# A windowed-attention block on one core: fc2 rows moved into the attention loop, value products for two pairs at once

## The reference

```
y   = layernorm(x) * g1 + b1, rolled by (-3, -3), cut into 64 windows of 49 tokens per image
qkv = y @ qkv_w.T + qkv_b                                  # 3 x 16 heads x 8
a   = softmax(q @ k.T / sqrt(8) + rel_pos_bias + shift_mask)
x1  = x + roll_back((a @ v) @ proj_w.T + proj_b)
out = x1 + (gelu((layernorm(x1) * g2 + b2) @ fc1_w.T + fc1_b)) @ fc2_w.T + fc2_b     # 128 -> 512 -> 128
```

## Time and profile before

| | us |
|---|---|
| median of three runs | 4173.44 |
| the profiled execution | 4173.6 |
| its span, first to last instruction | 4171.8 |
| PE busy | 3995.3 (96%) |
| DVE busy | 2933.7 (70%) |
| ACT busy | 2726.8 (65%) |
| POOL busy | 2122.9 (51%) |

### The profile page before, as it was taken

How to read it: one execution, slowest core, us unless ns; L and a number is a source line. 1 busy time by engine, 2 the same in 40 slices (tenths; PEclk the granted TensorE clock), 3 DMA queues, 4 the chain that set the end, 5 groups by cost and what they waited for, 6 DMA issues and landing times.

```text
span 4171.8 us, 170732 instructions
## 1 busy us (share of the span) xinstructions
PE 3995.3 (96%) x72080; PEld 3128.2 (75%) x72080; DVE 2933.7 (70%) x7196; ACT 2726.8 (65%) x5120; POOL 2122.9 (51%) x3476
## 2 busy tenths in 40 slices
PE   3899999999999999999999999999999999999998
PEld 2677777777777777777777777777777777777777
DVE  6677777777767777776777777777677767777774
ACT  1566666666666666666666666666666666666665
POOL 4455555555555555555555555555555455555553
PEclk8999999999999999999999999999999999999999
DMA  2333333333333333333333333333333333333332
GB/s 74 103 107 109 106 110 107 110 107 107 111 103 109 110 107 108 107 111 106 109 107 107 108 109 110 108 106 112 102 110 107 111 103 108 108 108 108 110 111 59
DMA packets 625966, 441.61 MB, mean 106 GB/s; under 512 B 158468, under 2 KB 624756, under 8 KB 625204
## 3 DMA queue, kind: packets, MB, share of 16 engines
q1 hardware_dynamic: 624739, 428.88, 34.8%
q0 software_dynamic: 464, 1.81, 0.1%
HBM read 106.14 MB, written 51.46 MB: 38 GB/s over the span
## 4 chain that ended last, share of the span: by engine, by line
PE 54%; ACT 16%; DVE 10%; issue 9%; DMA 7%; SPq 2%; ACTq 0%; POOL 0%; DVEq 0%; POOLq 0%
PE ps L766 13%; PE ps L718 10%; PE ps L796 9%; DMA sums<-pv_sb 7%; PE ps L753 7%; PE ps L748 6%; PE ps L780 6%; ACT hid L425 5%; ACT v_own L482 5%; DVE k_lo L615 3%; DVE yT_lo L600 3%; ACT probs L408 3%; ACT k_hi L466 2%; SPq L248 2%; DVE q_lo L615 2%
## 5 line engine op out<-in xcount | busy, mean ns | idle before, releaser
L570 DVE TENSOR_REDUCE neg_max<-ps 113x16 f32<-113x784 f32 x1024 | 993.1, 970 | 394.7 <-PE ps L718 386.1
L408 ACT ACTIVATE probs<-ps 113x784 f32<-113x784 f32 x1024 | 831.4, 824 | 492.8 <-PE ps L753 489.5
L796 PE MATMUL ps<-w,hid 128*112 128x128 f32 x7168 | 858.3, 274 | 0.0
L796 PEld LDWEIGHTS ps<-w,hid 128*112 128x112 f32 x7168 | 815.2, 177 | 21.9 <-issue 0.2
L753 PE MATMUL ps<-st_q,st_k 128*49 128x196 f16 x8192 | 700.9, 249 | 0.0
L748 PE MATMUL ps<-bias,eye_k 108*64 108x392 f16 x4096 | 689.8, 332 | 0.6 <-DMA bias<-neg_maxT 0.6
L425 ACT ACTIVATE hid<-ps,col 128x448 f32<-128x448 f32 (+1 forms) x1024 | 511.9, 576 | 231.1 <-PE ps L780 231.1
L766 PE MATMUL ps<-probs,v_own 113*32 113x49 f32 x32768 | 576.5, 210 | 45.0 <-ACT probs L408 34.3
L766 PEld LDWEIGHTS ps<-probs,v_own 113*32 113x32 f32 x32768 | 432.0, 109 | 227.7 <-issue 132.3
L378 POOL TENSOR_TENSOR x_b<-x,fc_b 112x896 f32<-112x896 f32 x128 | 267.7, 2091 | 604.4 <-DVE y_out L563 604.4
L718 PE MATMUL ps<-mx_k,mx_q 128*49 128x196 f16 x8192 | 548.7, 254 | 17.8 <-DMA mx_k<-k_hi 8.8
(11 more groups left out here) (108 smaller groups left out, 6962.8 us busy)
## 6 DMA issues: line engine op xcount, KB each, us to landing
st_k<-k_hi SPq DMA_DIRECT2D x256, 196.0 KB
st_q<-q_hi SPq DMA_DIRECT2D x1024, 49.0 KB
oT_raw<-pv_sb SPq DMA_DIRECT2D x256, 196.0 KB, 2.7
x_in<-in_x SPq DMA_DIRECT2D x224, 196.0 KB
x_res<-in_x SPq DMA_DIRECT2D x224, 196.0 KB
out_y<-y_out SPq DMA_DIRECT2D x224, 196.0 KB
mx_q<-q_hi SPq DMA_DIRECT2D x128, 196.0 KB
mx_k<-k_hi SPq DMA_DIRECT2D x512, 49.0 KB
```

Source lines behind the costliest of these rows:

```text
L408: nc.scalar.activation(probs[0:KP, w % 2, :].rearrange("p (b c) -> p b c", b=2), ps[0:KP, b:b + 2, 0:HB * WT], ACT.Exp).then_inc(s_exp, 1)
L570: nc.vector.tensor_reduce(neg_max[0:KP, :, w, :], ps[0:KP, 0:2, 0:HB * WT].rearrange("p b (h k) -> p b h k", k=WT), AX_X, ALU.max, negate= ...
L796: last = mm(tokens_of(6)[0:TP, i, :], hid[:, c, i * TP:(i + 1) * TP], w_2[:, c, :], start=(c == 0), stop=(c == CH - 1))
```

## The change

The mathematics stays the same. What moves:

- **fc2 and its evacuation.** `HALVES` is replaced for fc2 by `FC2_PARTS` = rows 0 to 2 and rows 3 to 6. Rows 3 to 6 of step t-2 run in the attention loop of turn t, one at each odd w, ahead of `max_logits`; rows 0 to 2 run in the head of the next turn. Each part uses bank 7 alone. The final addition of rows 3 to 6 is at the end of DVE's turn.
- **pv.** Two pairs' value products are one group of 32 matmuls in bank 6, at w = 2, 4, 6 and in the next head, with one copy of 392 columns instead of two of 196. Four probability buffers replace two.
- **The head's order.** The transposes of z are first, ahead of pv. Then come x's transposes, the maxima's, three fc2 rows, two fc1 groups, k, q, one fc1 group, the spread, the last fc1 group, v, the output projection. fc1 and gelu work on 784 columns in two banks, in four groups instead of eight. The k and q copies on ACT take both images at once.
- **yT.** The high part is written by ACT straight from PSUM, the low part by DVE from PSUM; the float32 copy and the cast on DVE go.
- **The row maxima in the logits.** They were two rows of the `bias` operand and are now the unused fourth row of each group of `st_q`, against ones in `st_k`; bias no longer has a copy for each w. The four DMAs of the maxima carry 32 pieces of 98 values each instead of 64 of 49.
- **SP.** The store `out_y` is issued after the maxima, ahead of `r_rows`, instead of after the logits' operands.
- **DVE.** `norm1` runs before k_lo and q_lo instead of after them.

```diff
@@ SP body
+                n = t - 3
+                if exists(n):
+                    sp.wait_ge(s_fin, 2 * (n + 1))
+                    band_dmas(sp, outr, y_out, n, edge(n), True, s_stored)
                 n = t - 1
                 if exists(n):
...
-                n = t - 3
-                if exists(n):
-                    sp.wait_ge(s_fin, 2 * (n + 1))
-                    band_dmas(sp, outr, y_out, n, edge(n), True, s_stored)
@@ ACT
+            def gelu(n, c):
+                if c == 0 and past(n, 0):
+                    act.wait_ge(s_fc2, 2 * n)
+                act.wait_ge(s_fc1, CH * n + c + 1)
+                bank = 2 + 2 * (c % 2)
+                nc.scalar.activation(hid[:, c, :].rearrange("p (b q) -> p b q", b=2), ps[:, bank:bank + 2, 0:HT],
                                      ACT.Gelu, bias=col[:, BF + c:BF + c + 1], scale=1 / W_SCALE).then_inc(s_gelu, 1)
...
                     for w in range(NW):
                         exp_pair(t, w)
-                        if w > 0:
-                            copy_pv(t, w - 1)
+                        if w % 2 == 0 and w > 0:
+                            copy_pv(t, w // 2 - 1)
@@ DVE body
                 if exists(t - 3):
                     finish(t - 3, 0, edge)
                 n = t + 2
                 if exists(n) and n != 0:
                     norm1(n, edge)
-                if exists(t - 3):
-                    finish(t - 3, 1, edge)
+                n = t + 1
+                if exists(n):
+                    for j, (hi, lo, bank, b) in enumerate(((k_hi, k_lo, 0, BK), (q_hi, q_lo, 6, BQ))):
+                        dve.wait_ge(s_hi, 2 * n + j + 1)
+                        for im in range(2):
+                            last = nc.vector.scalar_tensor_tensor(
...
+                if exists(t - 2):
+                    finish(t - 2, 1, edge)
@@ PE
+            def pv(n, u):
+                pe.wait_ge(s_exp, NW * n + 2 * u + 2)
...
+                for w in (2 * u, 2 * u + 1):
+                    for h in range(NH):
+                        g, r = h // NR, h % NR
+                        first = (2 * g + w % 2) * WT
+                        last = mm(ps[32 * r:32 * r + VC, 6, first:first + WT],
+                                  v_own[0:KP, w, h, :], probs[0:KP, w % 4, h * WT:(h + 1) * WT], start=True, stop=True)
...
+            def fc2(n, p, i):
+                first, end = FC2_PARTS[p]
+                if i == first and p == 1:
+                    pe.wait_ge(s_gelu, CH * (n + 1))
...
+                for c in range(CH):
+                    last = mm(ps[0:TP, 7, (i - first) * C:(i - first + 1) * C], hid[:, c, i * TP:(i + 1) * TP], w_2[:, c, :],
+                              start=(c == 0), stop=(c == CH - 1))
...
                 for w in range(NW):
                     if exists(t):
                         logits(t, w, edge, odd(0))
-                    if exists(t) and w > 0:
-                        pv(t, w - 1)
+                        if w % 2 == 0 and w > 0:
+                            pv(t, w // 2 - 1)
+                    if exists(t - 2) and w % 2:
+                        fc2(t - 2, 1, FC2_PARTS[1][0] + w // 2)
                     if exists(t + 1):
                         max_logits(t + 1, w, edge)
```

More of the change, by code:

```diff
@@ L261, in body @@
                     sp.wait_ge(s_negT, n + 1)
[L262 to L266, removed]
+                    for e in range(EQ):
+                        row = 32 * e + MAX_ROW
+                        sp.dma_start(st_q[odd(0)][row:row + 1, e, :, :].rearrange("p g c -> p (g c)"),
+                                     neg_maxT[32 * e:32 * (e + 1), :, :]).then_inc(s_neg_dma, 16)
+                n = t - 3
+                if exists(n):
+                    sp.wait_ge(s_fin, 2 * (n + 1))
+                    band_dmas(sp, outr, y_out, n, edge(n), True, s_stored)
                 n = t - 1
@@ L779, in fc1 @@
+            def fc1(n, c):
+                if c == 0:
+                    pe.wait_ge(s_h_lo, n + 1)
+                elif c == 1 and exists(n + 1):
+                    pe.wait_ge(s_exp, NW * (n + 2))
+                elif c > 1:
+                    pe.wait_ge(s_gelu, CH * n + c - 1)
+                bank = 2 + 2 * (c % 2)
                 for k, (ww, hh) in enumerate(((w1_hi, h_hi), (w1_hi, h_lo), (w1_lo, h_hi))):
-                    last = mm(ps[:, 2 + m % 4, 0:(i1 - i0) * TP], ww[:, c * C:(c + 1) * C], hh[:, i0 * TP:i1 * TP],
-                              start=(k == 0), stop=(k == 2))
+                    for b in range(2):
+                        last = mm(ps[:, bank + b, 0:HT], ww[:, c * C:(c + 1) * C], hh[:, b * HT:(b + 1) * HT],
+                                  start=(k == 0), stop=(k == 2))
@@ new lines, in body @@
+            def body(t, edge, odd):
+                n = t - 2
+                if exists(n):
+                    pe.wait_ge(s_z2, n + 1)
+                    if exists(t - 1):
+                        pe.wait_ge(s_exp, NW * t - 1)
+                    else:
+                        pe.wait_ge(s_gelu, CH * n)
+                    for i in range(WS):
+                        last = nc.tensor.transpose(tokens_of(2)[:, i, 0:TP], z2[:, i, :], idn[0:TP, 0:TP])
+                    last.then_inc(s_t2, 1)
@@ L802, in body @@
                 if exists(t - 1):
[L803 to L805 removed]
+                    pv(t - 1, NU - 1)
                 n = t + 1
@@ L815, in body @@
                     max_transposed(t)
-                n = t - 2
-                if exists(n):
-                    pe.wait_ge(s_z2, n + 1)
-                    if not exists(t - 1):
-                        pe.wait_ge(s_gelu, 2 * CH * n)
-                    for i in range(WS):
-                        last = nc.tensor.transpose(tokens_of(2)[:, i, 0:TP], z2[:, i, :], idn[0:TP, 0:TP])
-                    last.then_inc(s_t2, 1)
-                if exists(t - 3):
-                    fc2(t - 3, 2, 4)
+                if exists(t - 3):
+                    for i in range(*FC2_PARTS[0]):
+                        fc2(t - 3, 0, i)
@@ L839, in body @@
                 if exists(t - 2):
-                    for m in range(4):
-                        fc1(t - 2, m)
-                if exists(t - 3):
-                    fc2(t - 3, 4, WS)
+                    fc1(t - 2, 2)
                 n = t - 1
```

337 lines of the change are left out of this document (159 added, 178 removed).

## The result

The changed kernel takes **4627.6 us** (median of 4 runs, 4616.4 to 4649.1) against 4173.6 us: ratio 1.109, interval 1.107 to 1.111. It is 454 us slower. The forecast was 4795 us, range 4440 to 4930, slower. The profiled execution took 4637.0 us, with a span of 4635.2.

What follows compares the result with a forecast made beforehand. It took PE's own work to bound the loop, and put two chains' wait at the changed kernel's spread: 4173.6 + 124 x (3.24 turn + 1.8 clock) = 4799, say 4795 us; range 4440 to 4930, its own 4690 to 4930.

Steps and rivals of the forecast that it cites:

- PE ready for the spread at 10.3: In the head, PE finishes all work ahead of the spread 10.3 us into the turn.
- r_rows at 15.0: SP's chain to the spread: r_rows lands 15.0 us into the turn, including 3.7 to land and 0.6 for out_y ahead.
- The rule that I weighed: A DMA's semaphore lands after that engine's earlier writes: r_rows behind out_y, spread at 15.6, 0.5 us more per turn.
- k_lo at 15.6 (14.1 if x_in is early): DVE's chain to the spread: x_in at 12.3, statistics 2.07, k_lo 1.16; done at 15.6, or 14.1 with early x_in.
- The spread at 15.1: In the head, the spread starts 15.1 us into the turn (14.1 to 16.2), PE idling 4.8 us before it.
- The loop at 15.3: PE's attention loop with four fc2 rows in it takes 15.3 us per turn.
- The turn at full clock, 34.85: The whole turn without clock loss: 15.1 + 4.45 + 15.3 = 34.85 us, 3.2 more than before.
- The clock, 1.8 per turn: After the idle stretch at the spread, PE's lower clock adds 1.8 us per turn, bounds 1.7 and 5.
- The sum: Over 124 turns, 3.24 us of longer turn plus 1.8 for the clock adds 625 us.
- The same waits, the clock stays up: Rival: the spread waits as forecast but the clock does not fall; 4575 us (4450 to 4710), 36%.
- No wait, 3981: Rival: no wait at the spread, the loop and fewer gaps save 1.55 us per turn; 3981 us, 9%.
- the clock stays low, 5195: Rival: the clock stays low through the head and part of the loop, 5 us per turn; 5195 us, 6%.

Runs made afterwards that it cites:

- e1: The changed kernel with the store out_y put back behind the logits' operands on SP: 4540.8 us, ratio 1.087.
- e2: The changed kernel with the statistics of x_in put back behind k_lo and q_lo: 4668.4 us, median of three, ratio 1.116.
- e3: The changed kernel with both moves undone, out_y behind the logits' operands and the statistics of x_in behind k_lo and q_lo: 4321.0 us, ratio 1.035.
- e8: The kernel of e4 with the maxima's DMAs sent to two neighbouring unread rows of the value tile, maxima left out of the logits: 4890.9 us, one run.
- e4: The changed kernel with each of the four maxima's DMAs carrying 64 pieces of 98 bytes instead of 32 of 196: 4657.3 us, ratio 1.115.
- e5: The changed kernel with twelve superfluous fc1 matmuls, 2.0 us, added on PE just ahead of the spread: 4457.5 us, ratio 1.068.
- e10: The changed kernel with all seven fc2 rows in the head, rows 3 to 6 ahead of k, the others behind it: 4361.5 us, ratio 1.044.

## Why the prediction was right, and where its sizes were off

- **The number: inside the range, in part by luck.** 4628 is in 4440 to 4930, but outside 4690 to 4930, the range of the forecast itself; it lies in the part that was added for a rival whose premise is false. A loop 0.8 us too short in the sum also made up for a third of the 2.5 us by which the spread was put too late. Of the signs named, the idle of 4 to 5.5 us (2.6 in the median), DVE's wait of about 5 (2.4 in the turn shown), the loop steps of 1.97 and 2.12 (2.2 and 2.0) and the turn near 36.6 (35.0) did not come; the clock near 0.5 behind the spread did.
- **The mechanism: right.** PE waits at the spread in every turn, for two chains that end within half a us of each other, and in three of four turns the clock falls near the gap. "Undoing either alone would not help much" held in e1 and e2, and e3 shows that both were the cause.
- **PE ready for the spread at 10.3: right** (10.37). SP's start at 2.5: 2.36. From the spread to the loop 4.45: 4.44.
- **r_rows at 15.0: too late by 2.4. The step that failed is the landing.** The last issue came 8.17 after SP's start, 8.26 predicted. But r_lo landed 2.1 after its issue, not 3.7 plus 0.6 for `out_y`. The 3.7 was not r_rows' own. In the kernel before, the maxima's last transfer lands 3.4 us behind r_lo's issue, and in each of the turns 4 to 123 r_lo lands 0.31 to 0.76 us behind it, 0.37 in the median; from turn to turn the two move together (correlation 0.99). Their median in the view of the DMAs:

```profile
bias<-neg_maxT SPq DMA_DIRECT2D x512, 6.1 KB, 4.4
```

In the changed kernel the maxima land 0.5 us before r_lo is issued. In e8 they land 1.4 us behind its issue, which is less than the 2.0 that r_lo takes by itself, and it takes 2.2. No edit delays the maxima by 3 us and nothing else, so this is read from the traces and not shown by an experiment. The 0.6 for the store ahead was nothing, which these rows (changed kernel, then e1) show:

```profile
r_rows<-r_lo SPq DMA_DIRECT2D x128, 24.5 KB, 2.1
```
```profile
r_rows<-r_lo SPq DMA_DIRECT2D x128, 24.5 KB, 2.0
```

- The rule that I weighed, the Trainium skill, "DMA: Bandwidth & Descriptors", section "Queues, rings and completion order", would have made `r_rows` later behind `out_y`. Here it is later by what SP spends on issuing the store, 1.2 to 1.3 us (10.50 against 9.22), and by 0.1 us of landing. The runs don't contradict the rule: r_lo lands 0.4 us behind the last of `out_y` in the changed kernel, and behind the maxima in every turn of the kernel before. They show that the store came in time, so that its price was not paid here.
- **k_lo at 15.6 (14.1 if x_in is early): 12.24.** `x_in` was there 6.77 after SP's start, not 9.84, below the 8.3 that I had as the early end. Statistics and k_lo took 3.11, 3.23 predicted. I had the right suspect, the maxima's DMAs, by the wrong property: not their count (e4) but where they write (e8), which accounts for 1.5 us.
- **The spread at 15.1: 12.6.** It is below my 14.1, so the range of the wait was too narrow. PE idled 2.2, not 4.8.
- **The loop at 15.3: 16.1.** A row of fc2 is 1.06 by itself, not 0.91, and has a gap of 0.1 ahead of it like pv: odd w takes 2.22 (2018.79 to 2021.01), 1.97 predicted, four times; w = 0 takes 1.20, not 1.06. The even w are 1.97 to 2.03, not 2.12, since pv of two pairs is 0.83 (predicted 0.97). The average over 24 instructions in the earlier trace rows hid the fixed part.
- **The turn at full clock, 34.85: 33.13.** -2.5, 0 and +0.8.
- **The clock, 1.8 per turn: about right, for a wrong reason.** (536 - 51) / 2 / 124 is 1.96 at most, and e5 gave back 170 / 124 = 1.4. I had tied it to a gap longer than 3 us and took 2.55 us as harmless from one case. Here the gaps were 2.6 us in the median, and three of four turns had a low stretch; the 27 turns without one had gaps of 2.2 to 3.2. So the length of the gap alone doesn't decide it in this range.
- **The sum: 5.04 per turn, 3.58 measured.** The full-clock term carries the error, 3.24 against 1.52, and in it the wait, 4.8 against 2.2.
- **The rivals.** "The same waits, the clock stays up" gave 4575, nearer to the time than my forecast, but its premise is false: the clock fell. "No wait, 3981" and "the clock stays low, 5195" are refuted.

The Trainium skill's "TensorE: Matmul & The Clock Gate", section "HAM oscillation", describes a kernel that waits for a DMA in each tile and starts each one at the low clock. The trace agrees in the main: the clock was low near the spread in 93 of 120 turns.

## What to carry to other kernels

Before moving work out of the stretch ahead of a wait, sum the stretch that is left, and compare it with every chain that ends there, not only the one that is latest now: the cover is part of that work's value. Chains that end together must be shortened together, so test the edits in pairs before writing one off. And price a gap on PE twice, once for its length and once for the clock behind it.

## What the hardware showed that I had not expected

- Where many small pieces are written changes when a transfer beside them lands: `x_in` 8.67 against 7.19, the maxima 9.95 against 8.65 (e8, one run, and e4). The same bytes and pieces went to two neighbouring rows of one tile in e8 and to four rows 32 apart of another in e4; which difference counts is open. The view of the DMAs shows it in the maxima's own landing, 3.7 us from issue against 2.9; first e8, then e4:

```profile
v_own<-neg_maxT SPq DMA_DIRECT2D x512, 6.1 KB, 3.7
```
```profile
st_q<-neg_maxT SPq DMA_DIRECT2D x512, 6.1 KB, 2.9
```

- The same 24.5 KB transfer landed 3.7 us after its issue where the maxima's transfers were still under way for 3.4 us (the kernel before), and 2.1 where they had landed (the changed kernel).
- A block of float32 matmuls between fp16 ones has a fixed cost: 8 take 1.06 us and 24 take 2.62, so 0.78 for each further eight and 0.28 once, and 0.1 as a gap ahead (32 in e10 would be 3.40 by this and took 3.56).
- Idle stretches of 2.6 us in the median, once in a turn of 33 to 38 us, came with a lower clock for 3.4 or 6.8 us in 93 of 120 turns; with 1.1 us (e3) it was 14 of 120.
- Useless matmuls in such a gap made a kernel 170 us faster (e5).
